# One more step per unit by way of the turned path, in four units of a state-space scan kernel

## The chip, the cores and the metric

The kernel runs on one core of a Trainium2 chip. The metric is device time in microseconds. A core has TensorE (PE, matmuls and transposes; its weight loads are shown as PEld), VectorE (DVE), ScalarE (ACT), GpSimd (POOL) and SyncE (SP, which issues the DMAs here). They run side by side, each through its own instructions in order, and wait for each other by semaphores.

## What is computed

The input is `x`, 4 sequences of 512 tokens with 128 features. It is normalised, passed through two Mamba blocks (one forward, one on the reversed sequence), normalised and added; then a feed-forward part with a gate follows in the same manner. The core of a Mamba block is a recurrence over time for each of 256 channels and 16 states:

```
dA  = exp(dt[..., None] * A)
dBu = dt[..., None] * Bm[:, :, None, :] * u[..., None]
h = dA_t * h + dBu_t
y = einsum('bdn,bn->bd', h, C_t)          # sum over the 16 states
...
x = x + layernorm(attn(layernorm(x)))     # attn: x + forward + backward block
x = x + layernorm(ffn(layernorm(x)))      # ffn: (silu(x Wg) * (x Wu)) Wd
```

## The kernel before, in words

The work is cut in 8 units, numbered 0 to 7: a sequence and a direction each, forward in even units, backward in odd ones. A unit has 16 steps, one for each state, so there are 128 steps; step 1 of unit 4 is step 65 of all. A step treats 256 channels by 512 tokens, as a tile of 128 partitions by 1024.

A step needs these pieces:

- the decay: ACT makes `da = exp(dt * A)` in two instructions (L909), up to five steps ahead (ring of 6);
- the input term `dBu = dtu * B`, in one of three ways. *Plain*: PE spreads a row of B over the partitions into the PSUM tile `bb` (stage `bcast`, L652, one matmul), and DVE multiplies it there by `dtu` (stage `mul_b`, L1257). *Turned*: ACT multiplies a transposed copy of `dtu` by a column of B into `g` (stage `g`, L1020, four instructions), and PE transposes `g` back into both halves of `bb` (stage `g_turn`, L679, eight matmuls); DVE has nothing to multiply. *Pooled*: GpSimd multiplies (L1135) and the decay goes to PSUM instead;
- the scan: one DVE instruction for all of the recurrence (L1276), for every step;
- the product with C on GpSimd (`mul_c`, L1123, in place in `hq`);
- the fold: PE adds the product into `ysum`, transposed (`fold`, L707, eight matmuls).

Buffers tie these together. `bb` has 2 slots, so PE may fill the slot of step i only when scan i-2 is done. `hq` has 5 slots, so scan i waits for fold i-5, and that for `mul_c` of i-5. `g` has 2 slots. The first fold of a unit waits until ACT has copied `ysum` of the unit before (`y_out`, L949).

The order of all stages stands in one list made by the function `plan`. For each step it writes scan, `mul_c`, the filling of `bb` for the next step and its multiply; then the decays of the step five later, the fold of the step three earlier, and then what is woven into this slot: taps of the convolution (L781), the `z` projection (L791), the projection `xproj` (L802), gates, layer norms (L1037, L1052, L1055), the feed-forward part (L862, L873, L883) and the copy `o` (L1095). Each engine takes its stages out of this list, in its order. `TURNED` is the table of turned steps by unit, and `g_slot` says in which slot ACT makes `g`.

Of the kernel before, what the change touches and what calls it, by code (L numbers as in the profile page):

```python
# [24 lines left out]
DI, NS, RANK, TAPS = 256, 16, 8, 4  # L25
# [26 lines left out]
PARTS = 3  # L52


TURNED = ((4, 6, 10, 13), (2, 4, 6, 10, 13)) + 3 * ((3, 6, 10, 12, 15), (0, 5, 10, 13))
POOLED = ((15,), (15,), (8, 14), (15,)) + 2 * ((8, 14), (8, 15))
POOLED_RING = 2

# [18 lines left out]
def is_turned(i):  # L77

    return i % NS in TURNED[i // NS]

# [36 lines left out]
def plan():  # L117
# [4 lines left out]
    def put(slot, *items):  # L122
        woven[slot].extend(items)

    def taps(k, h):
        return [("tap", k, h, t) for t in range(TAPS)]
# [18 lines left out]
    for k in range(UNITS):  # L145
        q, d, n, at = k // 2, k % 2, k + 1, NS * k
        more, ffn = n < UNITS, d == 1 and q >= 1
        lag = 2 if k == 0 else 0
        z_slot = at + lag + 4 if more else at + 1
        g_slot = {2: 0, 3: 0, 4: 1, 5: 1, 6: 2, 10: 7 if k >= 2 else 6, 12: 9, 13: 8 if ffn else 10, 15: 11}  # L150
        for p in TURNED[k]:
            if p:
                put(at + g_slot[p], ("g", at + p))
        for p in POOLED[k]:
            put(at + {8: 4, 14: 10, 15: 11}[p], ("mul_b_pooled", at + p))
        if k == 0:
            put(at, ("dtu_turn", 0, 0), ("dtu_turn", 0, 1), ("pick",), ("split", 0), ("turn", 0, 1))
            put(at + 1, ("b_rows", 0))
            put(at + 8, ("neg_mean",), ("wo_sum",))
            put(at + 11, ("wo_centre",))  # L160
        if k == 1:
            put(at + 8, ("down_sum",))
            put(at + 11, ("down_centre",))

        if more:
            put(at + lag, *taps(n, 0)[:2])
            put(at + lag + 1, *taps(n, 0)[2:])
            put(at + lag + 2, *taps(n, 1)[:2])
            put(at + lag + 3, *taps(n, 1)[2:], ("conv_out", n, 0), ("conv_out", n, 1))
        put(z_slot, ("z", k, 0), ("z", k, 1))  # L170
        late[z_slot] = z_slot

        if k >= 1:
            put(at + 5, ("back", k - 1, 0))
            put(at + 6, ("gate", k - 1, 0), ("back", k - 1, 1))
            put(at + 7, ("gate", k - 1, 1))

        if more:
            put(at + 7, ("xproj_mm", n, 0), ("xproj_mm", n, 1), ("xproj", n))
            put(at + 8, ("bc", n))  # L180
            put(at + 9, ("dt_mm", n, 0), ("dt_mm", n, 1), ("dt", n, 0), ("dt", n, 1), ("split", n), ("dtu", n))

        if d == 0 and q >= 1:
            for b in range(BLK):
                put(at + 10 + b, ("oproj_mm", q - 1, 0, b))
            put(at + 13, ("oproj", q - 1, 0))
            put(at + 14, ("ln_square", 2, q - 1))
            put(at + 15, ("ln_var", 2, q - 1, 0), ("ln_pow", 2, q - 1, 0))
            put(at + 17, ("ln_act", 2, q - 1, 0), ("add_attn", q - 1, 0))
        if ffn:  # L190
            put(at + 3, ("ln_square", 3, q - 1))
            put(at + 4, ("ln_var", 3, q - 1, 0), ("ln_pow", 3, q - 1, 0), ("ln_shift", 3, q - 1, 0))
            put(at + 6, ("ln_act", 3, q - 1, 0))
            soon = 0 if more else -2
            sooner[at + 7].append(("turn_x1", q - 1, 0))
            put(at + soon + 10, ("ffn_gate", q - 1, 0, 0), ("ffn_gate", q - 1, 0, 1))
            put(at + soon + 11, ("ffn_gate", q - 1, 0, 2))
            late[at + soon + 10] = late[at + soon + 11] = at + soon + 11
            for c in range(3):
                sooner[at + soon + 12 + c].append(("ffn_up_mm", q - 1, 0, c))  # L200
                put(at + soon + 12 + c, ("ffn_up", q - 1, 0, c))
            put(at + soon + 15, ("ffn_down_mm", q - 1, 0, 0), ("ffn_down_mm", q - 1, 0, 1))
            put(at + soon + 16, ("ffn_down_mm", q - 1, 0, 2), ("ffn_down", q - 1, 0))
            soon += 0 if more else -1
            put(at + soon + 17, ("ln_square", 4, q - 1))
            put(at + soon + 18, ("ln_var", 4, q - 1, 0), ("ln_pow", 4, q - 1, 0))
            put(at + soon + 20, ("ln_act", 4, q - 1, 0), ("add_ffn", q - 1, 0))

        if more:
            put(at + (11 if ffn or k == 0 else 10), ("b_rows", n))  # L210
            soon = 1 if d == 0 and k >= 1 else 0
            put(at + 12 - soon, ("dtu_turn", n, 0))
            put(at + 13, ("dtu_turn", n, 1))
            if q < LAST:
                put(at + 14, ("turn", q + 1, d))
            if 0 in TURNED[n]:
                put(at + 14 - soon, ("g", at + NS))
    put(STEPS - 5, ("oproj_part_mm",), ("oproj_part",))

    ahead = {0: (3,), 1: (4, 5), 2: (6, 7)}  # L220
# [95 lines left out]

def mamba_sandwich(nc, x, packed, conv_taps, w_u, w_ffn, bc_rows, out):
    ORDER = plan()
    BANK = plan_banks(ORDER)

# [1179 lines left out]
```

How the kernel before makes its waits and increments, by code:

```python
        def may_write(eng, item):  # L475
            bank, n = BANK[item]
            if n > 1:
                eng.wait_ge(s_read[bank], n - 1)
# [1 line left out]
        def written(eng, item):  # L481
            bank, n = BANK[item]
            eng.wait_ge(s_full[bank], n)
# [1 line left out]
        def was_read(eng, item):  # L485
            bank, n = BANK[item]
            eng.wait_ge(s_read[bank], n)
# [28 lines left out]
        def dtu_ready(eng, k):  # L517
            if k == 0:
                eng.wait_ge(s_dtu_first, 2)
            else:
                eng.wait_ge(s_dtu, k)
# [1 line left out]
        def normed_ready(eng, q):  # L523
            if q == 0:
                eng.wait_ge(s_normed_first, 1)
            else:
                eng.wait_ge(s_normed, q)
# [1 line left out]
        def attn_in_ready(eng, q):  # L529
            eng.wait_ge(s_attn_in, INPUT_ORDER.index(q) + 1)
# [13 lines left out]
        def ln_in_ready(eng, w, q):  # L544
            if w == 3:
                eng.wait_ge(s_x1, q + 1)
            else:
                was_read(eng, made_by(w, q, 0))
# [1 line left out]
        def tail_ln_in_ready(eng, w, r):  # L551
            if w == 3:
                eng.wait_ge(s_tail_x1, turn_of(r) + 1)
            else:
                written(eng, made_by(w, LAST, r))
# [8 lines left out]
        def ln_ready(eng, w, q, r):  # L564
            if q == LAST and w != 3:
                was_read(eng, made_by(w, q, r))
            else:
                eng.wait_ge(s_norm[w - 2], q + 1 + (turn_of(r) if q == LAST else 0))
# [53 lines left out]
        @program.tensor  # L623
# [140 lines left out]
                elif stage == "u_raw":  # L764
                    pe.wait_ge(s_wu, 16)
                    pe.wait_ge(s_zero, 1)
```

## Time and profile before

| | |
|---|---|
| time, median of 3 runs | 463.37 us (463.2 to 463.65) |
| time of the profiled execution | 464.86 us |
| span of it, first to last instruction | 463.0 us |
| mean granted clock of TensorE | 0.939 of full |
| DVE, PE, POOL, ACT busy | 91%, 86%, 86%, 81% of the span |
| DVE scans (L1276) | 115 of 2.279 us and 13 of 2.273 us |
| POOL products with C (L1123) | 127 of 2.367 us |

All four engines are busy most of the time, and no share alone says which of them sets the pace. The pace is read where an engine waits: the number in brackets behind a row of the timeline is the idle time before the instruction, and what ended it. An instruction without a bracket followed the one before it on its engine at once. Rows of the timeline may stand for several instructions of one line (x8); their starts and lengths then cover them all.

### The profile page before, as it was taken

To read this page: it belongs to the slowest core of one execution; us is meant where nothing else is said; L and a number is where in the kernel's file an instruction comes from. 1 tells how busy PE (TensorE), PEld (TensorE's weight loads), DVE (VectorE), ACT (ScalarE), POOL (GpSimd) and SP (SyncE) were. 2 spreads that over 40 slices of the span, in tenths; PEclk is the share of its full clock that TensorE was granted. 3 is DMA by queue.
4 is the path that set the end of the run, shared out by engine and by line. 5 is a ranking of instruction groups with operands and counts; after the bars stand their busy time and mean duration, and the time that the engine had idled before them with its cause. 6 is when DMAs were issued, how large, how long until landed. Compare 5 with 4: busy or idle time off the path is not lost. (4 is left out here: it accounts for less than half of the span.)

```text
span 463.0 us, 6668 instructions
## 1 busy us (share of the span) xinstructions
PE 397.9 (86%) x2250; PEld 271.2 (59%) x2250; DVE 420.6 (91%) x338; ACT 374.6 (81%) x732; POOL 398.9 (86%) x239
## 2 busy tenths in 40 slices
PE   8769858997799799899998899799998882989973
PEld 3345545655656684565755675455765760758853
DVE  4999998899999999989999999989999998699744
ACT  4799997697868998988889998898889978783330
POOL 1689999878999899989989999989889999978521
PEclk9869997997899999989999999989999996799979
DMA  8542122222242213222233323122322323210001
GB/s 246 206 157 84 58 93 100 106 88 78 82 122 92 98 47 121 85 98 88 88 101 110 120 84 122 47 101 110 114 92 87 103 91 113 90 48 1 2 7 38
DMA packets 17777, 43.02 MB, mean 93 GB/s; under 512 B 1616, under 2 KB 7120, under 8 KB 17744
## 3 DMA queue, kind: packets, MB, share of 16 engines
q1 hardware_dynamic: 17744, 42.61, 26.9%
q8 instruction: 18, 0.29, 0.3%
q14 instruction: 15, 0.12, 0.1%
HBM read 41.03 MB, written 1.57 MB: 92 GB/s over the span
## 5 line engine op out<-in xcount | busy, mean ns | idle before, releaser
L1123 POOL TENSOR_TENSOR hq<-hq,c_tiles 128x1024 f32<-128x1024 f32 x127 | 297.8, 2367 | 23.5 <-DVE hq L1276 23.4
L1276 DVE TENSOR_TENSOR_SCAN hq<-da,bb 128x1024 f32<-128x1024 f32 x115 | 260.2, 2279 | 13.8 <-PE bb L679 5.1
L707 PE MATMUL ysum<-wts,hq 128*128 128x128 f32 x1024 | 143.2, 286 | 14.2 <-ACT y_t L949 8.0
L909 ACT ACTIVATE da<-dt,neg_a 128x511 f32<-128x511 f32 x230 | 149.5, 712 | 7.2 <-DVE hq L1276 7.0
L707 PEld LDWEIGHTS ysum<-wts,hq 128*128 128x128 f32 x1024 | 118.8, 146 | 39.5 <-issue 27.3
L1257 DVE TENSOR_TENSOR bb<-bb,dtu 128x1024 f32<-128x1024 f32 x79 | 95.6, 1210 | 4.5 <-PE bb L652 3.9
L1020 ACT ACTIVATE g<-dtu_t,bc_t 128x256 f32<-128x256 f32 x144 | 61.0, 500 | 0.5 <-ACT dtu_t L1008 0.5
L679 PE MATMUL bb<-wts,g 128*128 128x128 f32 x288 | 40.0, 284 | 4.0 <-DVE hq L1276 2.2
L679 PEld LDWEIGHTS bb<-wts,g 128*128 128x128 f32 x288 | 33.9, 146 | 13.0 <-issue 9.0
L652 PE MATMUL bb<-b_rows,pick 48*128 48x512 bf16 x75 | 29.8, 398 | 8.2 <-DVE hq L1276 8.2
L652 PEld LDWEIGHTS bb<-b_rows,pick 48*128 48x128 bf16 x75 | 7.0, 93 | 43.6 <-issue 25.3
L1135 POOL TENSOR_TENSOR dbu<-dtu,b_tiles 128x1024 f32<-128x1024 f32 x13 | 30.8, 2370 | 0.0
L781 PE MATMUL scr<-xn_rev,wconv 128*128 128x512 f32 x64 | 30.6, 600 | 0.0
L1276 DVE TENSOR_TENSOR_SCAN hq<-bb,dbu 128x1024 f32<-128x1024 f32 x13 | 29.5, 2273 | 0.8 <-issue 0.8
L781 PE MATMUL scr<-xn_fwd,wconv 128*128 128x512 f32 x56 | 28.1, 629 | 0.0
L1225 POOL TENSOR_TENSOR rstd<-rstd,minus_half 128x4 f32<-128x4 f32 (+1 forms) x15 | 13.8, 923 | 15.2 <-DVE rstd L1397 14.4
L873 PE MATMUL scr<-x_t,wffn 128*128 128x512 f32 (+1 forms) x46 | 22.6, 594 | 3.5 <-DVE hid L1432 1.5
L909 ACT ACT_TABLE_LOAD x17 | 21.8, 1283 | 0.4
L802 PE MATMUL scr<-u,wts 128*73 128x512 f32 x32 | 17.1, 662 | 0.6 <-ACT u L963 0.6
L949 ACT ACTIVATE y_t<-ysum 128x512 f32<-128x512 f32 x16 | 8.6, 589 | 10.2 <-PE ysum L707 10.2
L920 ACT ACTIVATE bb<-dt,neg_a 128x511 f32<-128x511 f32 x26 | 16.8, 677 | 0.0
L1212 POOL TENSOR_TENSOR dtu<-dt,u 128x1024 f32<-128x1024 f32 x7 | 16.6, 2366 | 0.1
(150 smaller groups left out, 484.2 us busy)
## 6 DMA issues: line engine op xcount, KB each, us to landing
c_tiles<-bc_rows_dram SPq DMA_DIRECT2D x64, 512.0 KB, 3.6
b_tiles<-bc_rows_dram SPq DMA_DIRECT2D x13, 256.0 KB, 4.4
x_res<-x_dram SPq DMA_DIRECT2D x1, 768.0 KB, 7.2
out_dram<-o SPq DMA_DIRECT2D x3, 256.0 KB, 2.3
wts<-packed_dram SPq DMA_DIRECT2D x1, 584.0 KB, 8.2
hid<-w_ffn_dram SPq DMA_DIRECT2D x1, 576.0 KB, 7.8
wconv<-conv_taps_dram SPq DMA_DIRECT2D x2, 256.0 KB, 4.2
wconv<-conv_taps_dram SPq DMA_DIRECT2D x1, 512.0 KB, 7.1
```

The lines of the kernel that those rows point to most:

```text
L652: mm = nc.tensor.matmul(bb[:, i % BB_RING, 1, :], pick[0:PARTS * NS, n:n + 1].broadcast_to([PARTS * NS, P]), b_rows[:, k % 2, :], start=Tr ...
L679: mm = nc.tensor.matmul(bb[:, i % BB_RING, h, block(b)], g[:, n % G_RING, b, h, :], ident, start=True, stop=True, is_transpose=True)
L707: mm = nc.tensor.matmul(ysum[:, bank, at], hq[:, i % H_RING, h, block(b)], ident, start=opens, stop=(i % NS == NS - 1), is_transpose=True, ...
L781: mm = nc.tensor.matmul(scratch(use), wconv[:, d, t, h * P:(h + 1) * P], src, start=(t == 0), stop=(t == TAPS - 1))
L802: mm = nc.tensor.matmul(scratch(use)[0:XROWS, :], wx[:, k % 2, h, :], u[:, k % U_RING, h, :], start=(h == first), stop=(h != first))
L873: signal_full(nc.tensor.matmul(scratch(use)[:, 0:at.stop - at.start], w[:, block(c)], x1_t[:, at], start=True, stop=True), use)
L909: ins = nc.scalar.activation(da[:, i % DA_RING, h, 1:SEQ], dt[:, k % 2, h, 1:SEQ], ACT.Exp, scale=neg_a[:, c:c + 1])
L1020: ins = nc.scalar.activation(g[:, m % G_RING, b], dtu_t[:, k % 2, b], ACT.Copy, scale=bc_t[:, k % 2, b, ROW_B + n:ROW_B + n + 1])
L1123: nc.gpsimd.tensor_tensor(hq[:, i % H_RING], hq[:, i % H_RING], c_tiles[:, n % C_RING, i % 2, :].unsqueeze(1).broadcast_to([P, 2, SEQ]), A ...
L1135: nc.gpsimd.tensor_tensor(dbu[:], dtu[:, k % 2], b_tiles[:, n % POOLED_RING].unsqueeze(1).broadcast_to([P, 2, SEQ]), ALU.mult).then_inc(s_ ...
L1257: nc.vector.tensor_tensor(bb[:, i % BB_RING], bb[:, i % BB_RING, 1, :].unsqueeze(1).broadcast_to([P, 2, SEQ]), dtu[:, k % 2], ALU.mult).th ...
L1276: nc.vector.tensor_tensor_scan(out=hq[:, i % H_RING].rearrange("p h t -> p (h t)"), data0=decay.rearrange("p h t -> p (h t)"), data1=dbu_t ...
```

## The change

Steps 3 of units 3 and 5 and steps 1 of units 4 and 6 (steps 51, 65, 83 and 97 of all) go from the plain to the turned way. Unit 2 keeps its table. In the units with a turned step 3 and a turned step 5, `g` of step 5 is made one slot later. As step 1 would have no slot of its own unit early enough, its `g` is put at the end of the unit before.

```
-TURNED = ((4, 6, 10, 13), (2, 4, 6, 10, 13)) + 3 * ((3, 6, 10, 12, 15), (0, 5, 10, 13))
+TURNED = ((4, 6, 10, 13), (2, 4, 6, 10, 13)) + ((3, 6, 10, 12, 15), (0, 3, 5, 10, 13)) + (
+    (1, 3, 6, 10, 12, 15), (0, 3, 5, 10, 13), (1, 3, 6, 10, 12, 15), (0, 5, 10, 13))
...
-        g_slot = {2: 0, 3: 0, 4: 1, 5: 1, 6: 2, 10: 7 if k >= 2 else 6, 12: 9, 13: 8 if ffn else 10, 15: 11}
+        g_slot = {2: 0, 3: 0, 4: 1, 5: 2 if 3 in TURNED[k] else 1, 6: 2, 10: 7 if k >= 2 else 6, 12: 9, 13: 8 if ffn else 10, 15: 11}
         for p in TURNED[k]:
-            if p:
+            if p > 1:
                 put(at + g_slot[p], ("g", at + p))
...
             if 0 in TURNED[n]:
                 put(at + 14 - soon, ("g", at + NS))
+            if 1 in TURNED[n]:
+                put(at + 15, ("g", at + NS + 1))
```

Three lines are added, so lines behind the second edit are numbered up to 3 higher in the changed kernel (L679 becomes L682, L1257 becomes L1260).

On PE, from the end of unit 3 into unit 4. In the order before, `bb<-b_rows,pick` is the spreading of a row of B, here for step 65 and then 66; `bb<-wts,g` is the turning back of step 67; `scr<-wffn,hid` is the feed-forward product for the copy `o`, `scr<-xn_rev,wconv` the taps:

```order
L883 MATMUL scr<-wffn,hid 128x128 x8
L652 MATMUL bb<-b_rows,pick 128x512
L707 MATMUL ysum<-wts,hq 128x128 x8
L883 MATMUL scr<-wffn,hid 128x128 x4
L781 MATMUL scr<-xn_rev,wconv 128x512 x2
L652 MATMUL bb<-b_rows,pick 128x512
L707 MATMUL ysum<-wts,hq 128x128 x8
L781 MATMUL scr<-xn_rev,wconv 128x512 x2
L679 MATMUL bb<-wts,g 128x128 x8
L707 MATMUL ysum<-wts,hq 128x128 x8
```

The same place in the changed kernel:

```order
L886 MATMUL scr<-wffn,hid 128x128 x8
L682 MATMUL bb<-wts,g 128x128 x8
L710 MATMUL ysum<-wts,hq 128x128 x8
L886 MATMUL scr<-wffn,hid 128x128 x4
L784 MATMUL scr<-xn_rev,wconv 128x512 x2
L655 MATMUL bb<-b_rows,pick 128x512
L710 MATMUL ysum<-wts,hq 128x128 x8
L784 MATMUL scr<-xn_rev,wconv 128x512 x2
L682 MATMUL bb<-wts,g 128x128 x8
L710 MATMUL ysum<-wts,hq 128x128 x8
```

One matmul has become eight; nothing else of the queue has moved. The place in unit 6 reads the same.

On ACT at that place, before (`g` here is the one of step 67; the four activations of `da` are the decays of steps 67 and 68):

```order
L909 ACTIVATE da<-dt,neg_a 128x511 x2
L954 ACTIVATE xn_rev<-scr,wts 128x512
L909 ACTIVATE da<-dt,neg_a 128x511 x4
L1095 ACTIVATE o<-scr 128x512
L1020 ACTIVATE g<-dtu_t,bc_t 128x256 x4
```

and in the changed kernel:

```order
L912 ACTIVATE da<-dt,neg_a 128x511 x2
L957 ACTIVATE xn_rev<-scr,wts 128x512
L912 ACTIVATE da<-dt,neg_a 128x511 x2
L1023 ACTIVATE g<-dtu_t,bc_t 128x256 x4
L912 ACTIVATE da<-dt,neg_a 128x511 x2
L1098 ACTIVATE o<-scr 128x512
L1023 ACTIVATE g<-dtu_t,bc_t 128x256 x4
```

The `g` of step 65 has come between the decays of steps 67 and 68.

On ACT at the start of unit 3, before (`ln_tile<-o,rstd` is L1052, which waits for GpSimd's `rstd`; `g` is that of step 53):

```order
L954 ACTIVATE xn_fwd<-scr,wts 128x512
L909 ACTIVATE da<-dt,neg_a 128x511 x6
L1052 ACTIVATE ln_tile<-o,rstd 128x128 x4
L1020 ACTIVATE g<-dtu_t,bc_t 128x256 x4
L909 ACTIVATE da<-dt,neg_a 128x511 x2
L949 ACTIVATE y_t<-ysum 128x512 x2
L909 ACTIVATE da<-dt,neg_a 128x511 x2
```

and in the changed kernel:

```order
L957 ACTIVATE xn_fwd<-scr,wts 128x512
L912 ACTIVATE da<-dt,neg_a 128x511 x4
L1023 ACTIVATE g<-dtu_t,bc_t 128x256 x4
L912 ACTIVATE da<-dt,neg_a 128x511 x2
L1055 ACTIVATE ln_tile<-o,rstd 128x128 x4
L912 ACTIVATE da<-dt,neg_a 128x511 x2
L952 ACTIVATE y_t<-ysum 128x512 x2
L1023 ACTIVATE g<-dtu_t,bc_t 128x256 x4
L912 ACTIVATE da<-dt,neg_a 128x511 x2
```

The new `g`, of step 51, stands ahead of the wait for `rstd`, and the `g` of step 53 now comes behind `y_t`.

## Rows read from the trace of the kernel before

**Rows 1.** Page, part 1: busy us, share of the span, instructions.

```profile
PE 397.9 (86%) x2250; PEld 271.2 (59%) x2250; DVE 420.6 (91%) x338; ACT 374.6 (81%) x732; POOL 398.9 (86%) x239
```

**Rows 2.** Page, part 5, a group: count, busy, mean ns, idle before, releaser.

```profile
L1257 DVE TENSOR_TENSOR bb<-bb,dtu 128x1024 f32<-128x1024 f32 x79 | 95.6, 1210 | 4.5 <-PE bb L652 3.9
```

**Rows 3.** Windows: stretch, length, busy (count) PE PEld DVE ACT POOL, PEclk, DMA, GB/s.

```profile
226.63:273.76 47.13, 43.88 (x286) 31.88 (x284) 46.02 (x27) 43.12 (x87) 44.76 (x26) 1.00 0.30 106
198.00:201.40 3.40, 3.40 (x12) 2.18 (x11) 3.40 (x3) 3.25 (x7) 3.40 (x3) 0.50 0.45 155
```

**Rows 4.** Timeline, unit 3: start us, us, engine, line, tiles, [idle before <-releaser].

```profile
179.40 1.28 ACT L1052 ACTIVATE ln_tile<-o,rstd 128x128 f32<-128x128 f32 x4 [2.06 <-POOL rstd L1225]
195.77 1.63 ACT L1055 ACTIVATE ln_tile<-x_res,shift,rstd 128x128 f32<-128x128 f32 x4
197.45 0.66 PE L862 MATMUL scr<-wts,ln_tile 128*128 128x128 f32 x4 [2.07 <-ACT ln_tile L1055]
199.61 2.77 PE L802 MATMUL scr<-u,wts 128*73 128x512 f32 x4
202.31 0.39 PE L652 MATMUL bb<-b_rows,pick 48*128 48x512 bf16 x1
202.74 1.23 DVE L1257 TENSOR_TENSOR bb<-bb,dtu 128x1024 f32<-128x1024 f32 x1 [1.12 <-PE bb L652]
```

**Rows 5.** Timeline, unit 5.

```profile
281.24 1.28 ACT L1052 ACTIVATE ln_tile<-o,rstd 128x128 f32<-128x128 f32 x4 [1.98 <-POOL rstd L1225]
297.96 1.65 ACT L1055 ACTIVATE ln_tile<-x_res,shift,rstd 128x128 f32<-128x128 f32 x4 [1.26 <-POOL shift L1231]
304.95 1.23 DVE L1257 TENSOR_TENSOR bb<-bb,dtu 128x1024 f32<-128x1024 f32 x1 [1.68 <-PE bb L652]
```

**Rows 6.** Timeline, end of unit 3 and unit 4.

```profile
223.80 1.33 ACT L909 ACTIVATE da<-dt,neg_a 128x511 f32<-128x511 f32 x2
226.00 0.39 PE L652 MATMUL bb<-b_rows,pick 48*128 48x512 bf16 x1
226.31 1.09 PE L707 MATMUL ysum<-wts,hq 128*128 128x128 f32 x8
228.34 0.60 ACT L1095 ACTIVATE o<-scr 128x512 f32<-128x512 f32 x1 [1.55 <-PE scr L883]
228.83 1.70 ACT L1020 ACTIVATE g<-dtu_t,bc_t 128x256 f32<-128x256 f32 x4
232.92 1.03 PE L679 MATMUL bb<-wts,g 128*128 128x128 f32 x8
233.79 1.04 PE L707 MATMUL ysum<-wts,hq 128*128 128x128 f32 x8
236.48 0.39 PE L652 MATMUL bb<-b_rows,pick 48*128 48x512 bf16 x1
238.01 1.21 DVE L1257 TENSOR_TENSOR bb<-bb,dtu 128x1024 f32<-128x1024 f32 x1
239.31 2.29 DVE L1276 TENSOR_TENSOR_SCAN hq<-da,bb 128x1024 f32<-128x1024 f32 x1
249.13 1.91 PE L802 MATMUL scr<-u,wts 128*73 128x512 f32 x4
257.54 2.37 POOL L1123 TENSOR_TENSOR hq<-hq,c_tiles 128x1024 f32<-128x1024 f32 x1 [0.43 <-DVE hq L1276]
```

**Rows 7.** Timeline, the same place of unit 6.

```profile
326.01 1.33 ACT L909 ACTIVATE da<-dt,neg_a 128x511 f32<-128x511 f32 x2
328.21 0.39 PE L652 MATMUL bb<-b_rows,pick 48*128 48x512 bf16 x1
338.69 0.39 PE L652 MATMUL bb<-b_rows,pick 48*128 48x512 bf16 x1
340.23 1.21 DVE L1257 TENSOR_TENSOR bb<-bb,dtu 128x1024 f32<-128x1024 f32 x1
```

**Rows 8.** Timeline, start of unit 7.

```profile
383.41 1.28 ACT L1052 ACTIVATE ln_tile<-o,rstd 128x128 f32<-128x128 f32 x4 [3.84 <-POOL rstd L1225]
```

## The prediction, made before the changed kernel was run

> **What bounds the kernel now.** I read the page's shares first [rows 1]. DVE is busy 91% of the span, PE and POOL 86%. That makes DVE look like the limit, but a share is a mean over places with different limits, so I asked next where DVE waits, and what the engines it waits for are waiting for, at the four places of the change.
>
> In unit 3, step 9 (step 57 of all), DVE stands idle 1.12 us until PE has spread B [rows 4]. Follow it back. PE spread it at 202.31, right behind the projection of 199.61 (2.77 us), which came behind the transpose L862 at 197.45. Before that one PE was idle 2.07 us, for ACT's L1055 at 195.77. ACT has no bracket there: it works without a pause from 179.40, where it had waited 2.06 us for POOL's `rstd`. So step 57 is set by POOL, then ACT, then PE, and not by DVE. In unit 5 it is the same [rows 5]: DVE waits 1.68 us at 304.95, and ACT waits for POOL both at 281.24 (1.98 us) and at 297.96 (1.26 us).
>
> From the end of unit 3 into unit 4 it is another engine. The copy `o` waits 1.55 us for PE [rows 6], while PE's own rows there have no bracket, from 226.00 to 238. PE spreads B for step 68 at 236.48, ready at 236.87, and DVE uses it at 238.01. That is 1.14 us of reserve, and only while DVE keeps its present pace. In unit 6 the same pair stands at 338.69 + 0.39 = 339.08 and 340.23, a reserve of 1.15 [rows 7].
>
> **The change, part by part.** Removed: four multiplies on DVE, 1.21 us each [rows 2]. From the start of such a multiply to the scan behind it the sum is about 1.3 us (the multiply at 238.01, its scan at 239.31 [rows 6]). With nothing else in the way each is worth 1.30 us.
>
> Added: four times four activations on ACT, 1.70 us a group [rows 6], and on PE eight transposes for one matmul. A turned filling keeps PE until its successor starts for 233.79 - 232.92 = 0.87 us, a spread for 226.31 - 226.00 = 0.31 us [rows 6]. So PE gets 0.56 us more each time. Nothing is added to POOL, SP or the DMAs.
>
> *Unit 3, step 3.* DVE is up to 1.30 us early from step 51 on. At step 57 it has to wait until PE has gone through the chain above, so its idle time of 1.12 us grows by what it gained. Would the chain itself come later? The new `g` goes into ACT's idle 2.06 us: ready at 179.40 - 2.06 = 177.34, plus 1.60 to the next start (1.70 less 0.1), is 178.94, still 0.46 before POOL's `rstd` at 179.40. The `g` of step 53 has gone behind `y_out`, and ACT does the same work after 179.40 as before. PE's 0.56 us are covered as well, by the idle 2.07 us before 197.45. Result: 0. The least gain here is 0, the most 1.30 if step 57 were free; I take 0, since the row shows who ends the wait.
>
> *Unit 5, step 3.* The same: 279.26 + 1.60 = 280.86, before 281.24. Result 0, with the same other end of 1.30.
>
> *Unit 4, step 1.* Here the new work meets a PE without reserve. ACT makes `g` of step 65 behind the decay that ends at 223.80 + 1.33 = 225.13. It starts 0.1 before that, takes 1.70, and is ready at 226.73 [rows 6]. PE would have started at 226.00 and now waits 0.73 us. With the 0.56 us from above, everything behind it on PE is 1.3 us later: fold 61, the product for `o`, the taps, and the spreads for 66 and 68. The idle 1.55 us of `o` hides the new `g` on ACT, but the `g` does not hide PE's delay: `o` is waiting for PE and moves with it. B for step 68 is then spread at 236.87 + 1.3 = 238.17, and the multiply can begin at 238.2, with the 0.04 us that row 202.74 shows after 202.31 + 0.39 [rows 4]. Before it began at 238.01. So the 1.30 us that DVE had gained at step 65 are gone by step 68, and 0.2 us more. After that PE is due again before DVE, and has reserve. POOL had been waiting 0.43 us for the scan of step 73 [rows 6], so this 0.2 reaches POOL too. POOL then paces the start of unit 5 [rows 5]. Result: +0.2 us. Its bounds: -1.30 (PE's delay costs nothing), and +1.3 (all of PE's delay reaches the scans through `y_out`, the `z` copies and the later `g`s, and is not made up).
>
> *Unit 6, step 1.* The same with its own numbers [rows 7]: `g` ready at 326.01 + 1.33 - 0.1 + 1.70 = 328.94 against 328.21, 0.73 late; plus 0.56 is 1.3; 339.08 + 1.3 + 0.04 = 340.4 against 340.23. Result +0.2, bounds as in unit 4. Unit 7 begins with ACT waiting 3.84 us for POOL [rows 8], so whatever POOL has lost or won by then is passed on whole.
>
> *The sum:* 0 + 0.2 + 0 + 0.2 = +0.4 us on the profiled execution's 464.86 us (span 463.0 and 1.86 around it), so 465.3. The median of the runs shown is 463.37, 1.5 below that execution; I put the difference on the median: 463.8 us.
>
> The Trainium skill, "Perfetto Trace Analysis", section "Identifying the Most-Contended Engine", says to optimise the engine of highest occupancy first. That is DVE, and by that rule the change is right; it is the first rival below. The rows at 202.74 and 304.95 speak against it for units 3 and 5.
>
> **The clock.** PE runs at full clock throughout unit 4, and at half in the 3.4 us from 198.00 [rows 3], just after the idle 2.07 us. There a projection takes 2.77 us, and 1.91 at full clock [rows 4, 6]; 0.86 us, and a fold beside it of 1.04 us at full clock [rows 6] can at most double. So such a stretch costs step 57 up to 1.9 us. In unit 5 PE gets 0.56 us more work and fewer idle microseconds. If that removes the slow stretch there, step 89 is up to 1.9 earlier; if one more appears, as much later. The Trainium skill, "TensorE: Matmul & The Clock Gate", "Part 4: PE-mode transpose", says that transposes do not count as PE being busy for the clock. By that the change, which puts eight transposes for one matmul, would rather lower it. The trace holds against a large effect: unit 4 has four or five turned fillings and folds that are all transposes, at 1.00.
>
> **The rivals.**
>
> 1. *DVE is the limit everywhere.* 4 x 1.30 = 5.2 us, 458.2 us. For it: 91%. Against it: the idle times in [rows 4, 5]. 4%.
> 2. *Units 3 and 5 give nothing, units 4 and 6 all.* PE's 1.3 us are caught up before step 68, since some of its apparent work is pipelined, and POOL, idle before step 73, follows. 2 x 1.30 = 2.6 us, 460.8 us. For it: POOL had idle time at 257.54 [rows 6], so it has room. Against it: no bracket on PE in [rows 6]. 10%.
> 3. *A half-clock stretch goes* in unit 3 or 5. 0.4 - 1.9 = -1.5, 461.9 us. 9%.
> 4. *PE's delay at steps 65 and 97 is passed on whole*, which is slower. Place: the wait for `g` of step 65, behind the decay at 223.80. Price: 0.73 + 0.56 = 1.3 us a unit, 2.6 in two, so 466.0 us. It decides if ACT, which gets `y_out` and `z` 1.3 us later, has no idle time left before the `g`s of steps 6 to 16; with half of that lost it would be 464.7. 22%.
> 5. *The forecast*: 463.8 us. 55%, within 463.0 to 464.6.
>
> **How the numbers follow.** A measurement of this kernel can tell about 0.2% from no change, 0.93 us: 462.4 to 464.3. Faster than that are rivals 1, 2 and most of 3: 0.22. Slower is rival 4 and the upper edge of the forecast: 0.25. The rest is 0.53. The range leaves out rivals 1 and 2 and part of what lies beyond 4: 461.7 to 466.0.
>
> **What the profile after will show.** If I am right: DVE's idle time at steps 57 and 89 is about 1.1 to 1.3 us longer than 1.12 and 1.68, with POOL's rows there at their old times; PE has a wait for `g` of about 0.7 us before the filling of steps 65 and 97, where it had none; `y_out` of units 3 and 5 is about 1.3 us late; the multiply of step 68 waits for PE; and POOL's products of steps 57 and 73 start at the old time and 0.2 us later. I am wrong if DVE starts step 73 by 0.5 us or more earlier than before (rival 2), if step 57 moves at all by more than 0.3 us, or if the stretches at half clock are others than before.

## The result, and the profile after

| | before | changed |
|---|---|---|
| median of 5 runs | 463.65 us (463.2 to 464.79) | 465.47 us (465.06 to 465.52) |
| ratio | | 1.0033, 95% interval 1.0017 to 1.0049 |
| profiled execution, span | 464.86, 463.0 us | 465.47, 463.7 us |

So in this measurement the changed kernel is slower by 0.33%. The ratio goes with the means of the executions rather than with the medians (for these five, 465.40 against 463.88 us). The forecast was +0.4 us; the two profiled executions differ by 0.6 us, the medians by 1.8. Two later measurements of the same changed kernel came out at 0.9965 and 0.9992. How that can be is most of what follows.

Part 1 of the page after, which answers to [rows 1]:

```profile
PE 403.7 (87%) x2278; PEld 277.5 (60%) x2278; DVE 417.0 (90%) x334; ACT 379.7 (82%) x748; POOL 398.7 (86%) x239
```

Four instructions less on DVE, 16 more on ACT, 28 more matmul instructions on PE. DVE has 3.6 us less to do, and the span is 0.6 us longer. What DVE was spared went into waits, as the group of multiplies shows, answering to [rows 2]:

```profile
L1260 DVE TENSOR_TENSOR bb<-bb,dtu 128x1024 f32<-128x1024 f32 x75 | 91.0, 1214 | 10.0 <-PE bb L655 9.5
```

The idle time ahead of these multiplies has grown from 4.5 to 10.0 us, 9.5 of it spent waiting for PE, where it was 3.9.

Unit 3 in the timeline of the changed kernel, answering to [rows 4] (all line numbers are 3 higher):

```profile
176.62 1.70 ACT L1023 ACTIVATE g<-dtu_t,bc_t 128x256 f32<-128x256 f32 x4
179.93 1.28 ACT L1055 ACTIVATE ln_tile<-o,rstd 128x128 f32<-128x128 f32 x4 [0.39 <-POOL rstd L1228]
196.29 1.63 ACT L1058 ACTIVATE ln_tile<-x_res,shift,rstd 128x128 f32<-128x128 f32 x4
197.98 0.66 PE L865 MATMUL scr<-wts,ln_tile 128*128 128x128 f32 x4 [2.06 <-ACT ln_tile L1058]
199.41 1.91 PE L805 MATMUL scr<-u,wts 128*73 128x512 f32 x4
201.26 0.39 PE L655 MATMUL bb<-b_rows,pick 48*128 48x512 bf16 x1
202.01 1.21 DVE L1260 TENSOR_TENSOR bb<-bb,dtu 128x1024 f32<-128x1024 f32 x1
```

The new `g` sits in ACT's hole: the wait for `rstd` is 0.39 us where it was 2.06. PE is idle for 2.06 us ahead of the transpose, as it was for 2.07. But the projection behind it takes 1.91 us and not 2.77, and step 57 is not held up. The wait that takes DVE's gain stands three steps earlier, at step 54. The first two rows are of the kernel before, the others of the changed one:

```profile
189.72 0.39 PE L652 MATMUL bb<-b_rows,pick 48*128 48x512 bf16 x1
190.22 1.21 DVE L1257 TENSOR_TENSOR bb<-bb,dtu 128x1024 f32<-128x1024 f32 x1
```

```profile
188.36 1.96 PE L794 MATMUL scr<-xn_fwd,wts 128*128 128x512 f32 x4 [0.33 <-ACT u L966]
190.25 0.39 PE L655 MATMUL bb<-b_rows,pick 48*128 48x512 bf16 x1
190.68 1.23 DVE L1260 TENSOR_TENSOR bb<-bb,dtu 128x1024 f32<-128x1024 f32 x1 [1.08 <-PE bb L655]
```

Before, B for step 54 was ready at 189.72 + 0.39 = 190.11 and used at 190.22. That is 0.11 us of reserve, which no bracket shows. Counted from the scan of step 48, PE's row has hardly moved (0.09 us earlier), so DVE, 1.32 us early by step 53, waits 1.08 us here. PE had itself been waiting for ACT's `u` (L966, L963 before).

The end of unit 3 and unit 4, answering to [rows 6]:

```profile
224.24 1.32 ACT L912 ACTIVATE da<-dt,neg_a 128x511 f32<-128x511 f32 x2
225.46 1.70 ACT L1023 ACTIVATE g<-dtu_t,bc_t 128x256 f32<-128x256 f32 x4
227.21 1.09 PE L682 MATMUL bb<-wts,g 128*128 128x128 f32 x8 [0.69 <-ACT g L1023]
228.14 1.04 PE L710 MATMUL ysum<-wts,hq 128*128 128x128 f32 x8
230.11 0.60 ACT L1098 ACTIVATE o<-scr 128x512 f32<-128x512 f32 x1 [1.73 <-PE scr L886]
238.25 0.39 PE L655 MATMUL bb<-b_rows,pick 48*128 48x512 bf16 x1
238.67 1.23 DVE L1260 TENSOR_TENSOR bb<-bb,dtu 128x1024 f32<-128x1024 f32 x1 [0.57 <-PE bb L655]
258.26 2.36 POOL L1126 TENSOR_TENSOR hq<-hq,c_tiles 128x1024 f32<-128x1024 f32 x1 [0.69 <-DVE hq L1279]
```

PE now waits 0.69 us for `g`, where it had no wait, and at step 68 it is DVE that waits 0.57 us for PE. POOL's wait for the scan of step 73 has grown from 0.43 to 0.69 us, so that scan is 0.26 us late for POOL too.

Unit 5, answering to [rows 5]:

```profile
281.91 1.28 ACT L1055 ACTIVATE ln_tile<-o,rstd 128x128 f32<-128x128 f32 x4 [0.24 <-POOL rstd L1228]
298.64 1.65 ACT L1058 ACTIVATE ln_tile<-x_res,shift,rstd 128x128 f32<-128x128 f32 x4 [1.02 <-POOL shift L1234]
302.95 3.55 PE L805 MATMUL scr<-u,wts 128*73 128x512 f32 x4
306.86 1.23 DVE L1260 TENSOR_TENSOR bb<-bb,dtu 128x1024 f32<-128x1024 f32 x1 [2.56 <-PE bb L655]
```

ACT starts L1058 0.68 us later than before, and the multiply of step 89 starts 1.9 us later, after waiting 2.56 us instead of 1.68. The projection takes 3.55 us: PE is at half clock here for longer. Windows of the changed kernel over its two stretches of half clock in units 3 and 5 (columns as in [rows 3]):

```profile
207.30:210.70 3.40, 3.40 (x10) 2.08 (x10) 3.31 (x3) 3.23 (x4) 3.15 (x7) 0.50 0.37 142
299.40:306.20 6.80, 5.86 (x16) 3.36 (x16) 3.22 (x3) 5.50 (x13) 6.80 (x4) 0.51 0.25 78
```

Before they were 3.4 us from 198.0 and 3.4 us from 300.4. Now the first falls on steps 58 to 60, the second is twice as long.

**Segment by segment.** The scan of each step is a good mark. For each segment between two scans I took how much longer it is than in the profiled execution of the kernel before (us). "To 48" is counted from the first scan, which starts at 22.7 to 23.1 us, and "end" is from the last scan to the end of the span:

| | to 48 | unit 3, 48-64 | 64-73 | 73-80 | unit 5, 80-96 | 96-105 | 105-127 | end | span |
|---|---|---|---|---|---|---|---|---|---|
| changed, first | +0.54 | -0.18 | +0.28 | +0.09 | +1.09 | +0.27 | -0.04 | -1.50 | 463.7 |
| changed, second | +0.29 | -1.07 | +0.29 | +0.10 | -0.19 | +0.28 | 0.00 | -3.04 | 459.6 |
| changed, third | -0.14 | -0.09 | +0.28 | +0.10 | -0.17 | +0.28 | -0.03 | -0.21 | 463.1 |
| steps 65, 97 only | +0.03 | -1.10 | +0.28 | +0.09 | -0.22 | +0.28 | -0.03 | -3.06 | 459.3 |
| steps 51, 83 only | -0.23 | -1.07 | 0.00 | -0.02 | -0.07 | 0.00 | -0.05 | -0.13 | 461.5 |
| `g` early, 65, 97 | +0.71 | -1.10 | -0.64 | +0.09 | -0.03 | -0.64 | -0.22 | -1.36 | 460.1 |
| the same again | -0.21 | -0.01 | -0.64 | +0.10 | +0.11 | -0.64 | -0.16 | -1.37 | 460.3 |
| `g` early, all four | -0.02 | -1.11 | -0.64 | +0.10 | -0.13 | -0.64 | -0.25 | -1.37 | 459.0 |
| before, PE load | -0.07 | -0.02 | +0.26 | +0.09 | -0.14 | +0.25 | -0.03 | -0.10 | 463.1 |
| changed, filled | -0.07 | +0.60 | +0.27 | +0.10 | -0.68 | +0.27 | -0.04 | -0.16 | 463.3 |
| before, filled | -0.76 | -1.01 | 0.00 | +0.01 | -0.23 | 0.00 | -0.03 | -0.15 | 460.9 |
| `g` early, unit 5 filled | +0.13 | +0.07 | -0.65 | +0.11 | +1.43 | -0.65 | -0.02 | -0.06 | 463.5 |

Two kinds of columns stand side by side. Where there is no half clock (64 to 73, 96 to 105) the numbers of kernels with the same edit there repeat to 0.01 us. The others, among them two in which nothing was changed (to 48, end), vary by up to 3 us between executions. Half clock does not cost the same everywhere: in 105 to 127 the first profile of the changed kernel has 13.7 us of it and the second 10.2, and their times differ by 0.04 us.

Step by step, the +0.28 of 64 to 73 is made up so. Counted from the scan of step 64, the spread for step 68 starts 1.32 us later than before (11.17 against 9.85), the multiply 0.21 later (11.59 against 11.38), and the scans from 71 on 0.27 later. In unit 3, all six profiles in which step 51 is turned have a gain of 1.32 us by step 53, a wait of 1.05 to 1.12 us for PE at step 54, and 0.07 to 0.17 us of gain left behind it; the others have no wait there. In unit 5 about half of the gain goes at step 86, where DVE waits 0.5 us for PE, and the rest at the scan of step 88.

### The profile page after: what moved, and what is told of

It reads as the page before. It is cut to its first block and busy times, and to the rows that moved or that the text cites. A ratio compares the mean times of both kernels' runs of the same rounds, so it can differ in the third digit from the quotient of the medians.

```text
span 463.7 us, 6748 instructions
## 1 busy us (share of the span) xinstructions
PE 403.7 (87%) x2278; PEld 277.5 (60%) x2278; DVE 417.0 (90%) x334; ACT 379.7 (82%) x748; POOL 398.7 (86%) x239
## 5 line engine op out<-in xcount | busy, mean ns | idle before, releaser
L710 PE MATMUL ysum<-wts,hq 128*128 128x128 f32 x1024 | 145.0, 288 | 11.7 <-ACT y_t L952 7.8
L710 PEld LDWEIGHTS ysum<-wts,hq 128*128 128x128 f32 x1024 | 120.9, 148 | 35.4 <-issue 26.1
L1260 DVE TENSOR_TENSOR bb<-bb,dtu 128x1024 f32<-128x1024 f32 x75 | 91.0, 1214 | 10.0 <-PE bb L655 9.5
L1023 ACT ACTIVATE g<-dtu_t,bc_t 128x256 f32<-128x256 f32 x160 | 67.7, 497 | 0.5 <-PE bb L682 0.5
L682 PE MATMUL bb<-wts,g 128*128 128x128 f32 x320 | 45.0, 287 | 5.1 <-ACT g L1023 3.4
L682 PEld LDWEIGHTS bb<-wts,g 128*128 128x128 f32 x320 | 38.1, 147 | 15.1 <-issue 8.5
L655 PE MATMUL bb<-b_rows,pick 48*128 48x512 bf16 x71 | 28.3, 399 | 6.0 <-DVE hq L1279 6.0
L784 PE MATMUL scr<-xn_rev,wconv 128*128 128x512 f32 x64 | 32.8, 638 | 0.0
L1228 POOL TENSOR_TENSOR rstd<-rstd,minus_half 128x4 f32<-128x4 f32 (+1 forms) x15 | 13.8, 922 | 13.7 <-DVE rstd L1400 12.9
L784 PEld LDWEIGHTS scr<-xn_rev,wconv 128*128 128x128 f32 x64 | 12.0, 208 | 9.5 <-issue 9.5
```

The source lines that it names most:

```text
L655: mm = nc.tensor.matmul(bb[:, i % BB_RING, 1, :], pick[0:PARTS * NS, n:n + 1].broadcast_to([PARTS * NS, P]), b_rows[:, k % 2, :], start=Tr ...
L682: mm = nc.tensor.matmul(bb[:, i % BB_RING, h, block(b)], g[:, n % G_RING, b, h, :], ident, start=True, stop=True, is_transpose=True)
L710: mm = nc.tensor.matmul(ysum[:, bank, at], hq[:, i % H_RING, h, block(b)], ident, start=opens, stop=(i % NS == NS - 1), is_transpose=True, ...
L784: mm = nc.tensor.matmul(scratch(use), wconv[:, d, t, h * P:(h + 1) * P], src, start=(t == 0), stop=(t == TAPS - 1))
L1023: ins = nc.scalar.activation(g[:, m % G_RING, b], dtu_t[:, k % 2, b], ACT.Copy, scale=bc_t[:, k % 2, b, ROW_B + n:ROW_B + n + 1])
L1260: nc.vector.tensor_tensor(bb[:, i % BB_RING], bb[:, i % BB_RING, 1, :].unsqueeze(1).broadcast_to([P, 2, SEQ]), dtu[:, k % 2], ALU.mult).th ...
```

## The experiments

**1. Steps 51 and 83 alone.**

```
-    (1, 3, 6, 10, 12, 15), (0, 3, 5, 10, 13), (1, 3, 6, 10, 12, 15), (0, 5, 10, 13))
+    (3, 6, 10, 12, 15), (0, 3, 5, 10, 13), (3, 6, 10, 12, 15), (0, 5, 10, 13))
```

> Only steps 51 and 83 (units 3 and 5) are turned as in the change. Theory (chain of POOL, ACT and PE sets steps 57 and 89): the 1.3 us that the scan of step 53 gains are lost by step 57, and unit 4 begins where it did, within 0.3 us; over the clock's doing, the time is that of the kernel before within 0.5 us (ratio 1.000). Clock theory (a stretch of half clock gets longer in unit 5, since PE starts the chain there a little later): the scan of step 89 is 1.0 to 1.9 us late in the profile, PE's clock is 0.5 for 6.8 us there instead of 3.4, and the time is +1.0 to +1.9 us, ratio 1.002 to 1.004. DVE as the limit: -2.6 us, ratio 0.994.

Measured: 463.67 us, ratio 1.0013 (0.9996 to 1.0030). In the profile unit 5 is -0.07 us, with 3.4 us at half clock as before. Unit 3 is -1.07, which looks like a gain. But this execution had no half clock in unit 3, and the next run, whose unit 3 is that of the kernel before, shows -1.10 for the same reason. So both steps are worth nothing, as forecast, though the gain of step 51 is lost at step 54 and not at step 57; that they lengthen the half clock in unit 5 is not borne out.

**2. Steps 65 and 97 alone.**

```
-TURNED = (...) + ((3, 6, 10, 12, 15), (0, 3, 5, 10, 13)) + (
-    (1, 3, 6, 10, 12, 15), (0, 3, 5, 10, 13), ...
+TURNED = (...) + ((3, 6, 10, 12, 15), (0, 5, 10, 13)) + (
+    (1, 3, 6, 10, 12, 15), (0, 5, 10, 13), ...
```

> Only steps 65 and 97 (units 4 and 6) are turned as in the change. Theory (PE's wait for g of 0.7 us and its 0.56 us more work use up the reserve at step 68): scan of step 73 is 0.2 to 0.3 us late and of step 105 0.4 to 0.6, time +0.5 us, ratio 1.001. Rival (PE's delay is passed on whole): +2.6 us, ratio 1.0055. If the clock is what made the changed kernel slow, this one stays below +0.7 us.

Measured: 461.64 us, ratio 0.9984 (0.9958 to 1.0009). By its steps it is +0.28 twice, just what the theory says. The whole time cannot show 0.5 us: eight of its executions lie between 460.5 and 462.7, four between 464.7 and 465.2.

**3. The same with `g` one slot earlier.**

```
             if 1 in TURNED[n]:
-                put(at + 15, ("g", at + NS + 1))
+                put(at + 14, ("g", at + NS + 1))
```

> As the run with steps 65 and 97 alone, but g of these steps is made one slot earlier on ACT (g ready at about 225.5 us, before PE is free at 226.0). Theory: the wait of 0.7 us on PE is gone, PE's delay at step 65 falls from 1.3 to 0.6 us, the spread for step 68 is ready at 237.5, and 0.5 to 0.6 us of DVE's gain are kept in each of units 4 and 6: time -1.0 to -1.2 us against the kernel before, ratio 0.9975. Rival (ACT has no room for g there, or PE's load alone takes the gain): no better than the run without the earlier slot, +0.5 us.

Measured: 461.89 us, ratio 0.9953 (0.9935 to 0.9970); units 4 and 6 each -0.64 us. The rows that decide it, from this run's timeline:

```profile
223.64 1.70 ACT L1023 ACTIVATE g<-dtu_t,bc_t 128x256 f32<-128x256 f32 x4
225.76 1.04 PE L682 MATMUL bb<-wts,g 128*128 128x128 f32 x8
236.74 0.39 PE L655 MATMUL bb<-b_rows,pick 48*128 48x512 bf16 x1
237.16 1.23 DVE L1260 TENSOR_TENSOR bb<-bb,dtu 128x1024 f32<-128x1024 f32 x1 [0.54 <-PE bb L655]
```

`g` is ready at 225.34, PE takes it at 225.76 without a bracket. At step 68 DVE still waits for PE, 0.54 us. So of the 1.30 us that DVE is spared, PE's 0.56 us more work takes about half even here. Taking away a wait of 0.69 us turned +0.28 into -0.64, that is 0.92 us. The spread for step 68 tells the same: counted from the scan of step 64 it was 1.32 us late in experiment 2 and is 0.40 late here. In the end of unit 6 and in unit 7 (105 to 127) the three profiles with the early `g` and no filling are 0.16 to 0.25 us shorter as well; why is not shown.

**4. The changed kernel with PE's idle time filled.** Ahead of the wait for the layer-norm tile (units 3 and 5), PE runs small matmuls into the bank that the transpose overwrites:

```
+                    may_write(pe, item)
+                    for _ in range({0: 8, 1: 13}.get(q, 0)):
+                        nc.tensor.matmul(scratch(item)[0:4 * SEQS * BLK]..., halves16, ...)
                     ln_ready(pe, 3, q, r)
-                    may_write(pe, item)
```

> The changed kernel with PE's idle time ahead of the transpose of the layer-norm tile in units 3 and 5 filled with 8 and 13 small matmuls (64 rows, 512 columns, bf16, 0.22 us apart at full clock) into the bank that the transpose overwrites. Clock theory: no stretch of half clock in steps 57 to 60 and 89, each worth 0.9 to 1.9 us, so 2 to 3.5 us less than the changed kernel: 462 to 463.5 us, ratio to before 0.996 to 0.999. Rival (the clock is not set by that idle time, or the steps wait for something else): 465.5 us as the changed kernel, or more if the filling holds the transpose up.

Measured: 464.18 us, ratio 1.0018 (0.9999 to 1.0038): the gain did not come. At step 89 there was no half clock, and the way from step 80 to 89 was 1.28 us shorter than in the profile of before. In unit 3 a stretch of half clock stood at 208.1, and the unit was +0.60. That the filling moved it there is not shown, since the first profile of the changed kernel has one at 207.3 without any filling. The rival that the filling holds the transpose up is true in part: in all ten profiles without filling in unit 5 the transpose starts 1.70 us behind the start of ACT's L1058 (L1055 before), and here 1.90.

**5. The kernel before with the same filling.**

> The kernel before with the same filling of PE's idle time in units 3 and 5. Clock theory: the stretch of half clock at step 89 goes (scan of step 89 about 1.2 us earlier than in the kernel before, counted from step 80), one in unit 3 may only move to steps 58 to 62: time -0.5 to -2 us, ratio 0.996 to 0.999. Rival (it does not matter to the clock): ratio 1.000.

Measured: 463.29 us, ratio 0.9998 (0.9975 to 1.0021). Its profile had no half clock in units 3 to 6 at all: unit 3 -1.01; step 80 to 89 -0.83, of which 0.60 were given back by step 96. The filling itself takes part of that. The first row is of the kernel before, the others of this run (L1059 is L1055, L866 is L862):

```profile
299.66 0.65 PE L862 MATMUL scr<-wts,ln_tile 128*128 128x128 f32 x4 [3.41 <-ACT ln_tile L1055]
```

```profile
295.80 2.99 PE L861 MATMUL scr<-minus_half 128*64 128x512 bf16 x13 [1.28 <-DVE gated L1385]
296.22 1.65 ACT L1059 ACTIVATE ln_tile<-x_res,shift,rstd 128x128 f32<-128x128 f32 x4 [1.25 <-POOL shift L1235]
298.72 0.66 PE L866 MATMUL scr<-wts,ln_tile 128*128 128x128 f32 x4
```

The small matmuls have to wait for DVE to free the bank, last until 298.7, and the transpose starts 2.50 us behind L1059 instead of 1.70: 0.80 us late. So not having the half clock is worth 1.0 to 1.1 us in unit 3, where the filling holds nothing up by more than 0.05 us. What it would be worth in unit 5 these runs leave open: experiment 4, held up by 0.2 us, is 1.1 us ahead of the third profile of the changed kernel at step 89 and 0.5 us at step 96. Over 12 executions nothing of it can be told.

**6. More load on PE alone.** In the kernel before, the spreading for steps 65 and 97 is followed by six repeats of itself:

```
+                        for _ in range(6 if i in (65, 97) else 0):
+                            mm = nc.tensor.matmul(bb[:, i % BB_RING, 1, :], ...)   # as above
```

> The kernel before with the spreading of B for steps 65 and 97 done seven times instead of once: 6 x 0.31 = 1.86 us more on PE, and nothing taken from DVE. Reserve theory: DVE has 1.14 us of reserve at step 68, so the scan of step 73 is 1.86 - 1.14 = 0.7 us late in unit 4, the same in unit 6, together +1.4 us, ratio 1.003. Whole passing-on: +3.7 us, ratio 1.008. If PE is not what counts there: 0.

Measured: 465.01 us, ratio 1.0000 (0.9970 to 1.0030). The median says little here, as the executions fall in two groups, five from 460.5 to 462.2 us and seven from 464.9 to 466.1; the means are 463.73 and, for the kernel before, 463.96. By its steps: +0.26 and +0.25 us in units 4 and 6. PE and DVE at that place:

```profile
225.77 0.39 PE L652 MATMUL bb<-b_rows,pick 48*128 48x512 bf16 x1
226.00 1.46 PE L656 MATMUL bb<-b_rows,pick 48*128 48x512 bf16 x6
227.38 1.09 PE L711 MATMUL ysum<-wts,hq 128*128 128x128 f32 x8
237.55 0.39 PE L652 MATMUL bb<-b_rows,pick 48*128 48x512 bf16 x1
```

My load was lighter than I had reckoned: the repeats are 0.2 us apart, and fold 61 starts 1.3 us after the time that it would have (227.38 - 225.77 = 1.61, less 0.31), not 1.86. That makes the run a better twin of the change than planned: the same 1.3 us on PE, DVE not relieved at all, and the same result, +0.26 against +0.28. What DVE is spared at step 65 is worth nothing while PE is that late.

**7. `g` early, with unit 5 filled.** The edits of 3 and 4, with 13 small matmuls in unit 5 only.

> The run with g one slot earlier (steps 65 and 97 alone turned) and 13 small matmuls in PE's idle time of unit 5. Theory: -1.3 us from the two units and 1.2 us from the stretch of half clock at step 89 that goes: 2 to 2.5 us less than before, 461 us, ratio 0.995. Rival: as without the filling, 461.9 us, ratio 0.9965.

Measured: 464.78 us, ratio 1.0009 (0.9986 to 1.0032). Units 4 and 6 are -0.65 each. Step 80 to 89 is -0.83, with the transpose held up by 0.94 us; then a stretch of half clock came at 311.0 and unit 5 ended at +1.43. A miss: the unit's half clock stood elsewhere, and the filling was in the way.

**8 and 9. The changed kernel a second and a third time.**

> The changed kernel once more, unchanged, beside the others. Its halves measured one by one give about +0.6 us (units 3 and 5) and -0.7 us (units 4 and 6) against the kernel before, but together they were +1.5 to +1.8 us. Theory (the steps cost +0.5 us and the rest is where the stretches of half clock fall, which differs from execution to execution): median 463.5 to 464.6 us, ratio 1.000 to 1.002. Rival (the two halves harm each other): again 465.3 us or more, ratio 1.0035.

> The changed kernel a third time, since its first two medians were 465.47 and 461.62 us. Theory (the change costs 0.6 us by its steps, and each execution draws its own stretches of half clock): times again spread over 460 to 466 us with a median between the two, profile +0.28 us in units 4 and 6 each. Rival (the first median was the true one): 465.3 us or more in most executions.

Measured: 461.62 us, ratio 0.9965 (0.9941 to 0.9989), and 461.34 us, ratio 0.9992 (0.9965 to 1.0019). The 29 executions of the changed kernel in all three measurements fall in two groups: 18 from 460.2 to 462.5 us, 11 from 464.9 to 465.7, and none between. The first measurement had all its five in the upper group. The 99 of the kernel before in the three later measurements lie from 461.3 to 465.6 us, median 463.45. The end of the kernel, from the last scan on, in windows of the kernel before, of the changed one in its first, second and third profile:

```profile
429.60:463.00 33.40, 22.82 (x132) 18.52 (x130) 17.82 (x58) 8.57 (x24) 9.92 (x10) 0.87 0.05 16
```

```profile
431.60:463.70 32.10, 21.44 (x132) 17.58 (x131) 17.96 (x58) 8.68 (x25) 9.92 (x10) 0.89 0.06 17
```

```profile
429.30:459.60 30.30, 19.66 (x132) 16.26 (x130) 17.73 (x57) 8.35 (x24) 9.95 (x10) 0.94 0.06 18
```

```profile
429.80:463.10 33.30, 22.66 (x132) 18.32 (x130) 17.89 (x58) 8.62 (x25) 9.92 (x10) 0.86 0.05 16
```

The same work takes 30.3 us at a mean clock of 0.94 and 33.3 at 0.86. From 443 us on and before a last stretch that all four have, the changed kernel's second profile has no half clock, its first has 3.4 us, its third and the kernel before have 6.8. None of the edits touches this part, and it is the largest difference in the table. The third profile has its half clock in units 3 and 5 where the kernel before has it (197.6 and 300.0, 3.4 us each). From step 48 to 127 it shows +0.37 us, which is the effect of the change with the clock of these units alike (in unit 7 it has 10.2 us of half clock where the kernel before has 13.7; that segment differs by 0.03).

**10. All four steps with `g` early**, and **11. experiment 3 again.**

> The changed kernel (steps 51, 65, 83 and 97 turned) with g of steps 65 and 97 one slot earlier. Theory (units 3 and 5 give nothing, units 4 and 6 -0.64 us each without PE's wait for g): scan of step 73 is 0.6 us earlier against step 64 than in the kernel before, the same in unit 6, steps 48 to 64 and 80 to 96 as before where the clock's stretches are the same; time -1.2 us apart from the clock, ratio 0.995 to 0.999. Rival (the steps of units 3 and 5 cost PE something that shows once unit 4 is tight): unit 4 gains less than 0.4 us.

> Steps 65 and 97 alone turned, g one slot earlier, once more. Theory (-1.3 us by its steps, the rest clock): ratio 0.995 to 0.999, and in the profile -0.64 us in unit 4 and in unit 6 again. Rival (the 0.9953 of the first time was all clock): ratio 1.000 or more.

Measured: 461.75 us, ratio 0.9979 (0.9960 to 0.9997), and 461.68 us, ratio 0.9972 (0.9955 to 0.9988). Both have -0.64 in units 4 and 6. Steps 51 and 83 add nothing to it. The version with steps 65 and 97 and the early `g` was faster than the kernel before in both of its measurements, and none of its 24 executions took over 463.2 us. Of its lead (2.2 us by the means the first time, 1.4 the second), 1.3 us are shown step by step in units 4 and 6; the rest is not. The last of these measurements and the third of the changed kernel shared a chip and the runs of before: ratios 0.9972 and 0.9992, whose intervals overlap. By its steps the version is 2 x 0.92 us better than the changed kernel.

## Why the prediction came out as it did

- *Units 3 and 5 give nothing: right, but for the most part not by the waits that I named.* They are worth 0 (experiments 1 and 10), and ACT's hole took the new `g`, with 0.39 us left where 0.46 had been worked out. But I had the gain last until steps 57 and 89 and the idle time there grow by 1.1 to 1.3 us. It did not, even with the half clock where it was before. These are steps 57 and 89 in the third profile:

```profile
202.54 1.23 DVE L1260 TENSOR_TENSOR bb<-bb,dtu 128x1024 f32<-128x1024 f32 x1 [1.16 <-PE bb L655]
304.97 1.23 DVE L1260 TENSOR_TENSOR bb<-bb,dtu 128x1024 f32<-128x1024 f32 x1 [1.32 <-PE bb L655]
```

  The waits were 1.12 and 1.68 us before, and are 1.16 and 1.32. The gain of step 51 had gone at step 54, that of step 83 at steps 86 and 88. Step 57's own wait is there only when a stretch of half clock stands ahead of it: in the eight profiles without one at 198, step 57 waits for nobody. Without such a stretch its B is ready about 0.5 us before it is used (200.65 + 0.39 = 201.04 and 201.57 in experiment 2), so with room at step 54 about that much of the gain would have come through, as an estimate. So the 0 of unit 3 was right by luck, through a reserve of 0.11 us that I had not looked for. I followed only rows that had a bracket before.
- *PE waits 0.73 us for `g` and is 1.3 us late: right.* 0.69 us, and the fold started 0.93 behind the turned filling. Against a spread in time that is 1.3 us. `y_out` of units 3 and 5 came 1.3 us late, as I had said.
- *+0.2 us in each of units 4 and 6: right in kind, a little small.* It was 0.27 to 0.29 in every trace that has this edit. The multiply of step 68 starts 0.21 us late, as worked out. It takes 1.23 us instead of 1.21, so that its scan is 0.24 us late; 0.03 us come on at step 71, and 0.1 us more from step 73 to step 80.
- *Rivals.* The first (DVE everywhere, 458.2) and the second (2.6 us gained) are out: experiments 1, 2 and 6. So is the fourth, that PE's delay is passed on whole: +0.28, not +1.3, and +0.26 with PE's delay alone. The second fell because PE's delay costs DVE all it has gained; with PE's wait taken away half of that gain does come. By its time alone the first measurement (465.5) lay nearer to the fourth rival (466.0) than to my forecast (463.8); only the segments tell them apart.
- *The sum: +0.4 by the steps, and +0.37 with the clock alike (third profile). The rest of the measured +1.8 us is not in the steps; I had put nothing in the sum for the clock.* I had written up to 1.9 us for one stretch of half clock in units 3 and 5 and given it to one rival on the faster side. It measured 1.1 us in unit 3, and such a stretch did go there, in six of the thirteen profiles; but at the end of the kernel, where I had looked for none, half clock moves the time by 3.0. The first profile differs from that of before by +0.54 up to step 48, +1.09 in unit 5 and -1.50 at the end. In unit 5 and at the end the half clock differs with it. Up to step 48 it does not account for the time: five profiles with stretches of the same lengths there lie from -0.02 to +0.71. And that profile itself was a slow draw: 464.86 us, with a median of 463.37 beside it. I corrected for the 1.5 us as an offset, and did not ask what they were. Stretches of half clock are the likely cause, but no other execution of the kernel before was traced, so that is not shown.
- So "faster, same or slower" was decided by something that my steps did not hold. The first measurement's interval (1.0017 to 1.0049) is narrow because its five executions were alike, not because the effect is; the second measurement's interval lies wholly below it, and the third's centre too. Over all 29 executions the mean is 462.8 us against 463.5 for the 99 of the kernel before, with a standard error of 0.4 us. That the change makes the kernel slower as a whole is not shown; that its steps cost 0.4 to 0.6 us in the traces is (+0.37 from step 48 to 127 in the third profile, 0.6 by the segments of units 4, 6 and 7 alone).
- A slip in the text on the change: the decays that stand around the new `g` there are those of steps 68 and 69, not 67 and 68. No number hangs on it.

Open: why the changed kernel falls in two groups of executions and the first measurement met only the upper one. Both groups occur in each of its later measurements, made on two different chips. Nor is it the change as a whole: steps 65 and 97 alone (8 and 4 executions) and the kernel before with more load on PE (5 and 7) fall in the same two groups, and what these have in common with it is PE's delay of 1.3 us in units 4 and 6. The 36 executions with the early `g` and no filling all stay below 463.4 us, but with unit 5 filled nine of twelve lie at 464.6 or above. Of these kernels, three of the four profiles from the upper group have 6.8 us of half clock at the end (from 443 or 444), and the fourth, the first of the changed kernel, has 3.4 there and 6.8 in unit 5; the two from the lower group have none at the end. That says what goes with the groups, not what brings it about.

## What to carry to other kernels

Work moved off the busiest engine gains only what the other engines' handovers behind it allow. For each piece that they hand to it, take the reserve: from the time when the piece is ready to the time when it is used. The first handover with less reserve than the saving takes what is above its reserve, even if the trace of before shows no wait there (step 54: 0.11 us of reserve, 1.32 us of gain, 0.13 left). Where the receiving engine gets a delay as well (here 0.73 us of wait and 0.56 of work), that comes off the reserve (1.14) first. If part of the delay is a wait, issue the producer earlier; one slot turned +0.28 into -0.64 us. And compare two traces in segments between fixed marks, so that what an edit does (0.01 us of scatter) is told apart from what the executions differ by anyway (3 us), before the median of a few executions is explained.

## What the runs showed of the hardware

- Executions of one kernel differ in where TensorE runs at half clock (1.2 instead of 2.4 GHz): the changed kernel's three profiles have different stretches. Over the 13 profiles of ten kernels the stretches are 3.4, 6.8, 10.2 or 13.7 us long, the one that the end of the program cuts off left aside. In unit 3 five profiles have one right behind PE's idle 2.1 us (at 198), two have one 10 us later, and six have none; in five of these six the same idle time stood there, unfilled.
- One of 3.4 us costs about 1.1 us in unit 3; at the end of the kernel, against the profiles with none from 443 to 451 us, 3.4 us go with 1.5 to 1.7 us and 6.8 us with 2.8 to 3.1; in steps 105 to 127 the difference between 13.7 and 10.2 us costs nothing that can be seen (0.04).
- In all ten profiles without filling in unit 5, half clock begins between 298.4 and 300.4 us; in the three with PE's idle time filled there, it does not, though one has it at 311.0. The filling brought no time in any of the three kernels, and in unit 5 it held up the work behind it by 0.2 to 0.9 us.
- In experiment 6 a repeat of a matmul with the same weights follows after 0.2 us; before, a spread is followed by another kind of matmul after 0.31.
